# Expert outputs: adding scatters into a token-ordered table in place of stores and gathers

## The reference

```python
def _L0_ffn_ref(x, W1, b1, W2, b2):          # x: the normalised tokens, 8192 x 128
    h = jnp.mod(x_flat[:, :TOP_K].sum(axis=1).astype(jnp.int32), E)
    sel = jnp.stack([h, jnp.mod(h + 1, E)], axis=1)
    def step(acc, params):
        e, W1e, b1e, W2e, b2e = params
        w = jnp.any(sel == e, axis=1).astype(x.dtype) / TOP_K
        y = jnp.maximum(x_flat @ W1e + b1e, 0.0) @ W2e + b2e
        return (acc + w[:, None] * y, None)
...
def _L0_attn_ref(x, ...):
    u = x @ W_x.T + b_x;  g = sigmoid(x @ W_g.T + b_g)
    h = depthwise_conv3(u) + conv_b
    u = u * g + h * (1.0 - g)
    dt = clip(softplus(x @ W_dt.T + b_dt).mean(axis=(0, 1)), 0.001, 2.0)
    A = -softplus(A_raw);  A_d = exp(A * dt[:, None]);  B_d = (A_d - 1.0) / (A + 1e-06) * B_ssm
    new = A_d[None] * carry + B_d[None] * u_t[:, :, None]     # scan over 256 steps
    y_t = einsum('bhs,hs->bh', new, C_ssm)
    return _layernorm(x + y @ W_out.T + b_out, ln_g, ln_b)
x = L0_attn_x;  xn = _layernorm(x)
return x + _L0_attn_ref(xn, ...) + _L0_ffn_ref(xn, ...)
```

## Time and profile before

| | before |
|---|---|
| executions, us | 517.22, 519.04, 520.28 |
| span of the profiled execution, us | 474.4 |
| time around the span, median less span | 44.6 |
| PE busy | 417.9 (88%) |
| DVE busy | 394.2 (83%) |
| ACT busy | 317.1 (67%) |
| POOL busy | 236.0 (50%) |
| moved by DMA | 52.77 MB |

### The profile page before, as it was taken

How to read it: one execution, slowest core, us unless ns; L and a number is a source line. 1 busy time by engine, 2 the same in 40 slices (tenths; PEclk the granted TensorE clock), 3 DMA queues, 4 the chain that set the end, 5 groups by cost and what they waited for, 6 DMA issues and landing times. The chain is left out here.

```text
span 474.4 us, 11853 instructions
## 1 busy us (share of the span) xinstructions
PE 417.9 (88%) x3387; PEld 368.2 (78%) x3387; DVE 394.2 (83%) x666; ACT 317.1 (67%) x898; POOL 236.0 (50%) x272
## 2 busy tenths in 40 slices
PE   1047999999899899999899999999998997999991
PEld 1035788887899899999899999899996544468881
DVE  6989666776559999999999999999972448995997
ACT  2686799998777677777566557665556664436873
POOL 4595777777424232222263354544312777676730
PEclk9999899999899999999999999999999999899996
DMA  9997334622221122212222134432211828179544
GB/s 236 261 414 263 102 116 114 181 73 81 86 55 33 33 46 43 42 35 44 62 67 44 33 92 129 94 73 46 44 38 44 223 62 220 46 196 253 163 127 133
DMA packets 111416, 52.77 MB, mean 111 GB/s; under 512 B 48881, under 2 KB 106393, under 8 KB 111385
## 3 DMA queue, kind: packets, MB, share of 16 engines
q1 hardware_dynamic: 106328, 43.48, 35.0%
q0 software_dynamic: 4096, 8.40, 5.9%
q10 hardware_dynamic: 960, 0.52, 0.4%
HBM read 28.12 MB, written 24.25 MB: 110 GB/s over the span
## 5 line engine op out<-in xcount | busy, mean ns | idle before, releaser
L1444 PE MATMUL PS<-AR 128*128 128x128 f32 x1184 | 140.1, 277 | 3.0 <-ACT AR L766 3.0
L1444 PEld LDWEIGHTS PS<-AR 128*128 128x128 f32 x1184 | 136.8, 194 | 3.6 <-ACT AR L766 3.6
L766 ACT ACTIVATE AR<-PS,VC 128x256 f32<-128x256 f32 x296 | 111.8, 488 | 4.2 <-PE PS L1432 3.0
L1430 PE MATMUL PS<-XT,RR 128*128 128x256 f32 x296 | 85.9, 290 | 3.6 <-POOL XT L579 3.4
L1431 PE MATMUL PS<-XT,RR 128*128 128x256 f32 x296 | 82.6, 279 | 0.0
L1432 PE MATMUL PS<-XT,RR 128*128 128x256 f32 x296 | 82.5, 279 | 0.0
L579 POOL TENSOR_TENSOR XT<-XTF,XT 128x256 fp32r<-128x256 f32 x35 | 31.2, 891 | 94.4 <-ACT XT L743 94.4
L573 POOL DMA_INDIRECT sorted_tokens<-RA,posi x64 | 63.0, 985 | 23.3 <-issue 11.6
L603 POOL TENSOR_TENSOR AR<-AR,b2p 128x256 f32 x37 | 33.9, 916 | 56.2 <-ACT AR L779 53.2
L1430 PEld LDWEIGHTS PS<-XT,RR 128*128 128x128 f32 x296 | 55.8, 188 | 5.3 <-POOL XT L579 4.9
L779 ACT ACTIVATE AR<-PS 128x128 f32 x74 | 16.6, 275 | 64.0 <-PE PS L1444 61.0
(11 more groups left out here) (230 smaller groups left out, 851.5 us busy)
## 6 DMA issues: line engine op xcount, KB each, us to landing
sorted_tokens<-AR SPq DMA_DIRECT2D x10, 512.0 KB, 5.6
XSIN<-sorted_tokens SPq DMA_DIRECT2D x160, 32.0 KB
sorted_outputs<-AR SPq DMA_DIRECT2D x37, 128.0 KB, 1.9
RA<-in_L_attn_x_dram SPq DMA_DIRECT2D x8, 512.0 KB, 8.0
normalised_tokens<-RA SPq DMA_DIRECT2D x16, 256.0 KB, 2.6
RB<-normalised_tokens SPq DMA_DIRECT2D x8, 512.0 KB, 7.5
AR<-in_L_ffn_W_dram SPq DMA_DIRECT2D x15, 256.0 KB, 3.6
out_dram<-RB SPq DMA_DIRECT2D x7, 512.0 KB, 3.3
```

Of the source, the lines that this page charges most:

```text
L766: nc.scalar.activation(HID[n][:, k, :], ps[2 * n + k // 2][:, (k % 2) * FT:(k % 2 + 1) * FT], ACT.Relu, bias=B1C[:, e, k:k + 1]).then_inc( ...
L1430: T.matmul(bank, W1h[slot][:, w], XT[:, 0:FT], start=True, stop=False)
L1444: ins = T.matmul(ps[5 + h][:, 0:D], HID[n][:, k, h * P:(h + 1) * P], W2S[slot][:, k, :], start=(n == 0 and k == 0), stop=(n == 1 and k == ...
```

## The change

`sorted_outputs`, its stores and its gathers go. A new DRAM table `expert_outputs` in token order (8192 rows and 896 spare ones) is filled with x by five DRAM-to-DRAM DMAs in the front. The rows of `sorted_tokens` become 144 floats: 128 of the token, its number as an integer, and 15 that are not used; in RA each token lies with its number behind it, 129 floats apart, and the scatter of line 573 sends 576 bytes per row. The rows that pad a group hold numbers of spare rows, written by the fill. For each tile SP loads the 256 numbers too. POOL copies them, adds the bias from YIN into YOUT (now one slot each in place of YSB's two), issues two adding scatters of 128 rows into `expert_outputs`, makes the low part of tile i+2, and waits until both scatters have landed before its next iteration. In the tail eight plain loads bring the eight tiles of the table into GA, as soon as the last scatter has landed; `add_x`, the loads of x and POOL's gathers are gone. `vrows` now lies in `bor`, to make room.

```diff
+    DX = 144
+    DI = D + 1
+    NPRE = 4
+    ZR = 2 * 512 // DX
+    NDUMP = ZR * P
+    NZ = ROWS // NDUMP
...
-        xs_dram = nc.dram_tensor("sorted_tokens", [ROWS, D], F32).ap()
-        ys_dram = nc.dram_tensor("sorted_outputs", [ROWS, D], F32).ap()
+        xs_dram = nc.dram_tensor("sorted_tokens", [ROWS, DX], F32).ap()
+        yt_dram = nc.dram_tensor("expert_outputs", [NTOK + NDUMP, D], F32).ap()
...
-        RA = sb("RA", [P, NTOK])
+        RA = sb("RA", [P, (NT - 1) * DI + DX])
+        XNI = RA[:, 0:NT * DI].rearrange("p (t d) -> p t d", d=DI)
+        XN = XNI[:, :, 0:D]
+        TOKEN = RA[:, 0:NT * DI].bitcast(I32).rearrange("p (t d) -> p t d", d=DI)[:, :, D]
...
-        YSB = AR[:, 8 * CH:9 * CH]
+        YIN = AR[:, 8 * CH:8 * CH + FT].rearrange("p (h d) -> p h d", h=FH)
+        YOUT = AR[:, 8 * CH + FT:9 * CH].rearrange("p (h d) -> p h d", h=FH)
...
@@ sync, front
+                sp.dma_start(xs_z[n], ZERO[:, 0:ZR * DX]).then_inc(s_fill, 16)
-            for n in range(NY):
-                ...
+            for b in range(NPRE):
+                bs = slice(b * (B // NPRE), (b + 1) * (B // NPRE))
+                sp.dma_start(yt_dram[b * (NTOK // NPRE):(b + 1) * (NTOK // NPRE), :],
+                             x[bs].rearrange("b l d -> (b l) d")).then_inc(s_pre, 16)
+            sp.dma_start(yt_dram[NTOK:NTOK + NDUMP, :], x.rearrange("b l d -> (b l) d")[0:NDUMP, :]).then_inc(s_pre, 16)
@@ sync, load_tile
+                ids = xs_i[t] if isinstance(t, int) else xs_i[bass.ds(t, 1)].rearrange("o p h d -> p (o h) d")
+                sp.dma_start(id_slot(t).rearrange("p (h o) -> p h o", o=1), ids, allow_slow_non_contiguous=True).then_inc(s_ids, 16)
@@ sync, expert loop
+                    sp.wait_ge(s_ids, i * 16 + 3 * 16)
...
                     load_tile(i + 3)
-                    sp.wait_ge(s_yad, i + 1)
+                    sp.wait_ge(s_idc, i + 1)
-                    sp.wait_ge(s_yst, i * 16 + 32)
-                    sp.dma_start(ys_v[bass.ds(i, 1)].rearrange("o p h d -> p (o h) d"), tile_of(YSB, i)).then_inc(s_yst, 16)
@@ sync, tail
-            sp.wait_ge(s_yst, bounds[E] * 16 + 32)
+            sp.wait_ge(s_mat, 1)
+            sp.wait_ge(s_osc, bounds[E] * (16 * FH))
-            for n in range(NAR):
-                load_x(n)
+            for n in range(NB8):
+                load_base(n)
...
@@ gpsimd, block scatter
-                    nc.gpsimd.indirect_dma_start(out=xs_dram, in_=XN[:, t, :], in_offset=None,
+                    nc.gpsimd.indirect_dma_start(out=xs_dram, in_=RA[:, t * DI:t * DI + DX], in_offset=None,
@@ gpsimd, expert loop
                 with pool.Fori(bounds[g], bounds[g + 1]) as i:
+                    pool.wait_ge(s_ids, i * 16 + 16)
+                    nc.gpsimd.tensor_copy(idx[:, :], id_slot(i)).then_inc(s_idc, 1)
                     pool.wait_ge(s_ysb, i + 2)
-                    nc.gpsimd.tensor_tensor(tile_of(YSB, i), tile_of(YSB, i), b2p..., ALU.add).then_inc(s_yad, 1)
+                    nc.gpsimd.tensor_tensor(YOUT, YIN, b2p..., ALU.add).then_inc(s_yad, 1)
+                    pool.wait_ge(s_idc, i + 1)
+                    pool.wait_ge(s_yad, i + 2)
+                    for h in range(FH):
+                        nc.gpsimd.indirect_dma_start(out=yt_dram, in_=YOUT[:, h, :], in_offset=None,
+                                                     out_offset=bass.IndirectOffsetOnAxis(ap=idx[:, h:h + 1], axis=0), compute_op=ALU.add
+                                                     ).then_inc(s_osc, 16)
                     with pool.If(i >= NLOW - 2):
                         with pool.If(i < bounds[E] - 1):
                             low_part(i + 2)
+                    pool.wait_ge(s_osc, i * (16 * FH) + 16 * FH)
@@ gpsimd, tail
-            for n in range(NB8):
-                for t in range(TB8):
-                    ...
-                    nc.gpsimd.indirect_dma_start(out=GA[n][:, t, :], out_offset=None, in_=ys_dram, ...
@@ scalar, expert loop
-                    act.wait_ge(s_yst, i * 16 + 16)
+                    act.wait_ge(s_yad, i + 1)
@@ vector, tail
-                if hb == 0 and n >= NB8 - NAR:
-                    dve.wait_ge(s_xb, n - (NB8 - NAR) + 1)
-            def add_x(n):
-                ...
-                V.tensor_tensor(GA[n], GA[n], XB[n], ALU.add).then_inc(s_xb, 1)
...
-                dve.wait_ge(s_xb, n + 1)
+                dve.wait_ge(s_gat[n], 16)
```

More of the change, by code:

```diff
@@ L156, in ssm_moe_layer @@
         tsi = sb("tsi", [P, E], I32)
+        NID = 4
+        idr = sb("idr", [P, NID * FH], I32)
+        idx = sb("idx", [P, FH], I32)
         consts = sb("consts", [P, 4])
@@ L233, in ssm_moe_layer @@
         ps = [PS[:, n, :] for n in range(8)]
-        XB = [batch(RC[:, 1, :], NB8 - NAR + n) for n in range(NAR)] + [batch(RB[:, 0, :], n) for n in range(NB8 - NAR)]
         def vpsum(t):
@@ L265, in ssm_moe_layer @@
         s_xnd = sem("normalised_tokens_stored")
-        s_xg = [sem(f"x_for_base_{n}") for n in range(8)]
-        s_xb = sem("x_added_to_outputs")
         s_actl = sem("last_log_ready")
@@ L321, in ssm_moe_layer @@
         s_yad = sem("expert_bias_added")
-        s_yst = sem("expert_output_stored")
+        s_tok = sem("token_numbers_ready")
+        s_pre = sem("x_copied_for_outputs")
+        s_ids = sem("token_numbers_of_tile_loaded")
+        s_idc = sem("token_numbers_of_tile_in_place")
+        s_osc = sem("expert_output_scattered")
         s_inj = sem("injection_ready")
@@ L328, in ssm_moe_layer @@
         s_ytr = sem("y_piece_transposed")
-        s_gat = [sem(f"expert_outputs_gathered_{n}") for n in range(NB8)]
+        s_gat = [sem(f"expert_outputs_loaded_{n}") for n in range(NB8)]
         s_xr = [sem(f"x_reloaded_{n}") for n in range(NB8)]
@@ L441, in _ @@
             sp.wait_ge(s_xs, 16 * NQ)
+            sp.wait_ge(s_ids, 16)
             load_tile(1)
@@ L447, in _ @@
             sp.wait_ge(s_xs, 2 * 16 * NQ)
+            sp.wait_ge(s_ids, 2 * 16)
             load_tile(2)
@@ L504, in _ @@
                 load_xn(n)
-            for n in range(NAR, NB8):
-                load_x(n)
             for n in range(NB8 - 1):
@@ L519, in _ @@
         def _(pool):
-            nc.gpsimd.memset(ZERO, 0.0).then_inc(s_zero, 1)
+            pool.sem_inc(s_yad, 1)
+            nc.gpsimd.memset(ZERO, 0.0).then_inc(s_tok, 1)
+            pool.wait_ge(s_tok, 1)
+            nc.gpsimd.iota(ZERO[:, 0:ZR * DX].bitcast(I32).rearrange("p (r d) -> p r d", d=DX)[:, :, D], [[1, ZR]], base=NTOK,
+                           channel_multiplier=ZR).then_inc(s_zero, 1)
             nc.gpsimd.iota(jv[:, :], [[1, Q + 1]], base=0, channel_multiplier=0,
@@ L540, in _ @@
                                ).then_inc(s_iot, 1)
+            nc.gpsimd.memset(RA[:, NT * DI:], 0.0).then_inc(s_tok, 1)
+            nc.gpsimd.iota(TOKEN, [[P, NT]], base=0, channel_multiplier=1).then_inc(s_tok, 1)
             pool.wait_ge(s_wraw, 64)
@@ L563, in _ @@
             pool.wait_ge(s_pos, 1)
+            pool.wait_ge(s_tok, 3)
             pool.wait_ge(s_fill, 16 * NZ)
@@ L592, in _ @@
                 if g >= 1:
-                    pool.wait_ge(s_yad, bounds[g])
+                    pool.wait_ge(s_yad, bounds[g] + 1)
                 nc.gpsimd.tensor_tensor(b2p[:, :], b2s[:, g % 3, :], b2s[:, (g + 1) % 3, :], ALU.add).then_inc(s_b2, 1)
@@ L776, in _ @@
                     act.wait_ge(s_m2, i + 1)
-                    act.wait_ge(s_yst, i * 16 + 16)
+                    act.wait_ge(s_yad, i + 1)
                     for h in range(FH):
-                        ins = nc.scalar.activation(YSB[:, bass.ds((i & 1) * FT + h * D, D)], ps[5 + h][:, 0:D], ACT.Copy, scale=0.5)
+                        ins = nc.scalar.activation(YIN[:, h, :], ps[5 + h][:, 0:D], ACT.Copy, scale=0.5)
                     ins.then_inc(s_ysb, 1)
@@ L1309, in _ @@
             add_base(3)
-            add_x(5)
             gain(4)
```

70 lines of the change are left out of this document (20 added, 50 removed).

## The result

| | before | after |
|---|---|---|
| executions, us | 517.22 to 523.73, median 519.66 | 581.99 to 591.08, median 583.70 |
| ratio, 95% interval | | 1.120 [1.113, 1.127] |
| span of the profiled execution, us | 474.4 | 580.3 (time 581.99) |
| PE, DVE, ACT, POOL busy, us | 417.9, 394.2, 317.1, 236.0 | 450.6, 383.7, 319.2, 304.6 |

A forecast was written before the change was run, and what follows sets the result against it. PE was taken to set the pace, DVE close behind, with POOL inside each tile's chain. Terms -5.9 - 1.7 - 1.4 + 0 + 12.0 + 3 + 0 = +6.0 us gave span 480.4, forecast 525.0 us, range 511 to 550.

The forecast's parts named there:

- Ordinary tile: Expert-stage tile without a change of expert: two adding scatters and their landing fit POOL's spare time, cost 0.
- The landing's range: Time from an adding scatter's start until it has landed: taken as 3.0 us, bounds 2.3 and 7.0.
- rival 2: Adding DMA slow in every tile; from a 3.5 us landing PE follows POOL; +32, 551 us; chance 0.16.
- Changes of expert: Expert stage, where weights are split: the landing is on POOL's path, cycle 8.94 us instead of 7.38; +12.0 us.
- Start and gating stage: First low part queued behind four scatters, and POOL's DMAs slowed beside DVE from 118 to 275 us: +3, 0 to +12.
- The front: Before the expert stage: larger fills, copy of x into the table and longer rows cost 0, up to +5 us.
- rival 3: Copy of x keeps DMA engines full, scatters land late: +8 at the first bias add, 530 us; chance 0.07.
- State stage: In the tail, without gathers and adds of x, six steps fall back to PE's pace: -5.9 us.
- Last batch: End of the output stage: DVE starts it at 466.0 instead of 467.7; -1.7 us, between -1.1 and -1.9.
- SP's load: Last tile load goes out earlier, shortening PE's 2.13 us wait at 364.20: -1.4 us, between 0 and -2.1.
- The sum's base: Profiled span 474.4 us plus 44.6 us up to the 519.04 median, left unchanged in the forecast.

## Why the prediction was wrong

**The step that failed: "Ordinary tile", with a sum of 0.** From the bias add of one tile to that of the next, POOL's chain held 0.75 (bias add) + 0.30 (gap) + 1.25 (the first scatter and the gap behind it) + 3.0 (landing, from the second one's start) + 0.6 (copy and waits) = 5.9 us, below PE's 6.37, so that "a landing up to 3.5 us costs nothing". In the tile shown above it is 0.74 + 0.79 + 1.97 + 4.61 + 0.14 = 8.25 us, and POOL, not PE, sets the pace. Three terms were too small: the gap behind the bias add by 0.5 (it is there with plain scatters too, which fit even so), the scatter instruction by 0.7, and the stretch from the second scatter's start to the next copy by 1.1 to 1.2; it is 3.87 us where nothing else covers it and 3.9 to 5.0 behind a low part. I had taken both durations from plain DMAs, though the trace of before had no adding one. The landing's range did reach 7.0, but rival 2, which is what happened, priced landing and instruction each alone, at 551 us, and it had a chance of 0.16; the loss measured, 64 us and 80.6 with a timely front, is twice its 32 and more. That the prices of the two scatters add up is shown by the two runs with one adding scatter. The Trainium skill, DMA: Bandwidth & Descriptors, Rules for kernel authors, says that an accumulating DMA reads its destination and writes it later. The longer landing agrees with that (3.2 us at least with both adding, 2.3 at least where one of the two is plain), but no run shows that the read is what takes the time.

**Changes of expert, +12.** The cycle forecast at 8.94 us was measured at 10.5 and 12.1. On one chip the seven intervals up to tiles 25 to 30 and 19 add 25.3 and 7.6 us. So this place costs 32.9 us where +12 was forecast. The size was off by the same durations. With plain scatters and two slots, where no landing stands in it, the cycle is still 8.5 to 8.9 us (297.21 to 306.15, 314.70 and 323.16, with waits for ACT of at most 0.96): there I had counted the landing and not the queue's own length.

**Start and gating stage, +3.** On time the start alone is +19.3 us; of these 9 are the copy's delay of POOL (the same four intervals take 43.6 us with it and 34.5 without it, with plain scatters). Of the gating stage I had the upper end for the case that each scatter is held off by DVE. The Trainium skill, SBUF — State Buffer, Who interferes with whom, says that a DVE instruction with two SBUF inputs contends with a GpSimd instruction that reads SBUF; that this reaches every scatter was my own step, and the section itself reports a probe in which such an instruction did not stall a DMA. The trace of two plain scatters without the copy doesn't bear out such a price: its W2 products of tiles 4 to 17 span 88.4 us, against 86.8 to 88.9 in two traces of the kernel before.

**The front, 0.** PE's front is not delayed, but with a timely front the token scatters end 6 to 10 us later with the copy (b2p at 128.17 without it, 134.38 to 138.08 with it), worth 7.8 us at the end. That is rival 3's place and price, and its mechanism shows too: landings of token scatters took 2.3/2.5/10.1 us with the copy (least, median, most) and 2.3/2.3/4.4 without it, in the two runs with plain scatters. The fills grow by an eighth, 1.5 us and not 1.4, which changes nothing.

**What was right.** State stage: -5.9 forecast, 50.09 to 43.84 measured, -6.3 (on one chip 49.12 to 43.84, -5.3). Last batch: -1.7 forecast, -1.5 measured. SP's load has the right sign only: -1.4 forecast, but PE's wait went from 2.13 to 1.77, -0.4. The three together are 8.1 us of the 9.0 that I had counted; they are a tenth of the loss.

**The sum's base.** The 44.6 us "around the span" were 1.7 us and a front that ran later on another chip. Held against its own profiled execution the forecast was 474.4 + 6 + 1.7 = 482; on that kind of chip the change gives 558.8.

Where the 80 us go on a chip with the front on time, by differences of the medians: plain scatters with one slot +23 (501.3 - 478; the tail's gain of 7 is in it), the copy +8 (509.1 - 501.3), adding +50 (558.8 - 509.1). Of the last the expert stage shows 21 for the first instruction and 28 for the second with its low part and landing. The four kernels ran on two chips, on which the kernel before takes 477.83 and 478.21 us.

## What to carry to other kernels

An operation that the trace of before doesn't hold is no row of its plain relative: when it stands twice in the loop of an engine that has 0.95 us to spare, measure it alone first, and price its instruction, its landing and the waits ahead of it together, not one at a time. An idle share of two thirds on an engine says nothing of the cycle in which it answers another; and work that wins 7 us in a tail must not be paid in a loop of 37 turns. Before a median and a profiled span are compared, see that both are of the same chip.

## What the runs showed of the hardware

- An adding indirect DMA of 128 rows of 512 bytes holds POOL for 1.55 us at least, 1.64 in the median, a plain one for 0.96 and 1.00; with 64 rows the adding one still takes 1.41 at least. It makes 144 packets on the queue, the plain one 32.
- Its landing took 3.2/3.4/4.9 us from the instruction's start (least, median, most), with the low part ahead of the scatters.
- A POOL instruction right behind it is stretched: the low part took 1.30 us in the mean, and 0.81 behind a plain scatter.
- A copy of 4.65 MB from DRAM to DRAM issued at 35.8 us did not delay PE's first W2 product, but the end of POOL's 64 indirect scatters, by 6 to 10 us.
- The changed kernel's first W2 product came at 119.3 us on one chip and at 157.0 on two occasions elsewhere; variants of it came at 148.6 to 156.5 there.
